# Issuing one tile's projections ahead of the previous tile's recurrence in a delta-rule attention layer

## What is computed

```python
q = silu(x @ Wq); k = l2_norm(silu(x @ Wk)); v = x @ Wv      # x: layer-normed
gk = log_sigmoid(x @ Wf1 @ Wf2)                              # per feature
gamma = -sigmoid(x @ Wgamma)                                 # per head
a = k * gamma[..., None] * exp(gk)
def step(S, inp):                                            # one token, per head
    qt, kt, vt, at, gkt = inp
    S = S * exp(gkt)[..., None]
    sab = einsum('bhk,bhkv->bhv', at, S)
    S = S + kt[..., None] * (sab[..., None, :] + vt[..., None, :])
    return (S, einsum('bhk,bhkv->bhv', qt, S))
o = scan(step) * sigmoid(x @ Wog1 @ Wog2); attn = norm(o) @ Wo
h = silu(x @ w1) * (x @ w2); h = gelu(h @ h1); h = gelu(h @ h2); ffn = h @ w3
out = x0 + attn + ffn
```

## Time and profile before

| | us |
|---|---|
| median of two timed runs | 13573.28 (13356.49 and 13790.07) |
| the profiled execution, device time | 13088.1 |
| its span, slowest core (core 2) | 13086.6 |
| spans of the eight cores | 13047.5 to 13086.6 |

### The profile page before, as it was taken

One profiled execution on the slowest core, in us unless ns is written; L12 is line 12 of the kernel. 1 busy time (PEld: TensorE's weight loads), 2 busy tenths in 40 slices (PEclk: granted clock), 3 DMA queues, 4 the chain that ended last, 5 costly groups with the idle time before them and its releaser, 6 DMA issues.

```text
span 13086.6 us, 179913 instructions; the slowest of 8 cores (13047.5 to 13086.6 us)
## 1 busy us (share of the span) xinstructions
PE 9249.0 (71%) x54234; PEld 4170.1 (32%) x55296; DVE 2440.8 (19%) x7011; ACT 2919.9 (22%) x8979; POOL 252.6 (2%) x479
## 2 busy tenths in 40 slices
PE   2566666666656656656656656699799799799577
PEld 0223223223223223223223223344344344344223
DVE  5222222222222222222222222000000000000222
ACT  1223323323333333333333333101010000000000
POOL 0000000000000000000000000000000000000110
PEclk5555555555555555555555555799999899899788
DMA  2100000000000000000000000322322322322421
GB/s 56 27 13 11 15 13 11 15 13 10 15 13 10 15 13 11 15 13 11 14 13 10 14 15 10 90 57 58 97 57 58 95 58 58 96 58 59 112 86 58
DMA packets 355161, 482.25 MB, mean 37 GB/s; under 512 B 162705, under 2 KB 277394, under 8 KB 336850
## 3 DMA queue, kind: packets, MB, share of 16 engines
q0 software_dynamic: 45040, 201.91, 8.3%
q10 hardware_dynamic: 177122, 235.20, 5.5%
q1 hardware_dynamic: 132096, 33.56, 1.4%
HBM read 479.50 MB, written 125.83 MB: 46 GB/s over the span
## 4 chain that ended last, share of the span: by engine, by line
PE 63%; ACT 11%; issue 10%; DVE 10%; DMA 3%; ACTq 2%; DVEq 1%; another core or an unknown queue 0%; POOL 0%; SPq 0%; POOLq 0%
PE lh_ps0h2t L1027 7%; PE lh_ps0h1t L1027 7%; PE lh_ps1h2t L1027 7%; PE lh_ps1h1t L1027 7%; PE p_ps L512 6%; PE p_px L855 6%; PE p_ps L521 5%; PE p_ps L560 3%; PE f_pF L1148 3%; PE p_pg L829 2%; ACT p_sumb L898 2%; DMA p_fmp<-p_pack 2%; DVE p_S L948 1%; DVE p2l_h L538 1%; ACT p2l_t L532 1%
## 5 line engine op out<-in xcount | busy, mean ns | idle before, releaser
L512 PE MATMUL p_ps<-xn_fm,p2l_wbb 128*128 128x512 bf16 x1775 | 1074.5, 605 | 375.9 <-DMA p_fmp<-p_pack 319.3
L521 PE MATMUL p_ps<-xn_fm,p2l_wbb 128*128 128x512 bf16 x1681 | 1023.2, 609 | 0.0
L1027 PE MATMUL lh_ps0h1t<-lh_hblkh1t,lh_wbbh1t 128*128 128x512 bf16 x4014 | 902.9, 380 | 150.4 <-DMA lh_hblkh1t<-h_dram 145.8
L1027 PE MATMUL lh_ps0h2t<-lh_hblkh2t,lh_wbbh2t 128*128 128x512 bf16 x4014 | 905.2, 381 | 140.5 <-DMA lh_hblkh2t<-g_dram 135.8
L1027 PE MATMUL lh_ps1h2t<-lh_hblkh2t,lh_wbbh2t 128*128 128x512 bf16 x4014 | 899.8, 379 | 4.4
L1027 PE MATMUL lh_ps1h1t<-lh_hblkh1t,lh_wbbh1t 128*128 128x512 bf16 x4014 | 899.8, 379 | 4.3
L863 ACT CAST p_xw<-p_px 128x128 bf16<-128x128 f32 x1280 | 340.6, 266 | 2011.7 <-PE p_px L855 2011.7
L1114 DVE TENSOR_SCALAR f_stats<-f_pS 1x512 f32<-1x512 f32 x8 | 5.4, 679 | 4087.1 <-DMA f_g2b<-h_dram 3915.2
L841 DVE CAST p_pow<-p_pg 128x128 bf16<-128x128 f32 x1280 | 373.2, 292 | 1989.8 <-PE p_pg4b L833 1989.8
L1027 PEld LDWEIGHTS lh_ps0h1t<-lh_hblkh1t,lh_wbbh1t 128*128 128x128 bf16 x4096 | 401.8, 98 | 631.4 <-issue 151.0
L1027 PEld LDWEIGHTS lh_ps0h2t<-lh_hblkh2t,lh_wbbh2t 128*128 128x128 bf16 x4096 | 402.4, 98 | 623.7 <-issue 144.6
(11 more groups left out here) (205 smaller groups left out, 12897.4 us busy)
## 6 DMA issues: line engine op xcount, KB each, us to landing
lh_wbbh1t<-h1t POOLq DMA_DIRECT2D x64, 1024.0 KB, 9.1
lh_wbbh2t<-h2t POOLq DMA_DIRECT2D x64, 1024.0 KB, 9.2
h_dram<-p2l_h ACTq DMA_DIRECT2D x256, 128.0 KB
lh_hblkh1t<-h_dram ACTq DMA_DIRECT2D x64, 512.0 KB
g_dram<-lh_gouth1t ACTq DMA_DIRECT2D x256, 128.0 KB
lh_hblkh2t<-g_dram ACTq DMA_DIRECT2D x64, 512.0 KB
h_dram<-lh_gouth2t ACTq DMA_DIRECT2D x256, 128.0 KB
f_g2b<-h_dram POOLq DMA_DIRECT2D x256, 128.0 KB, 5.3
```

The costliest lines, as they stand in the source:

```text
L512: kb.emit("tensor", lambda e, dc=dc, t0=t0, first=(dc == 0): e.matmul(ps4[:, 0:512], l1_wbb[:, dc * 128: dc * 128 + 128], xn[:, dc * T + t ...
L521: kb.emit("tensor", lambda e, dc=dc, t0=t0, first=(dc == 0): e.matmul(ps4[:, 512:1024], l1_wbb[:, 1024 + dc * 128: 1024 + dc * 128 + 128], ...
L1027: kb.emit("tensor", lambda e, dc=dc, b=b, pb=pb, ts=ts, TT=TT, first=(dc == 0): e.matmul(psb[pb][:, :], wbb[:, b * 4096 + dc * 128:b * 409 ...
```

## The change

The body of the tile loop is cut in two functions, `prologue(tk4)`, which returns the DT count of the transpose, and `waves(tk4, dtf)`. A new loop at the end of the segment calls them with the prologue one tile ahead. No instruction is added or removed, and no buffer is added. The order of the parts in a segment becomes head, P0, P1, W0, P2, W1, P3, W2, W3. The guards in `fr` are filled in at the time of each call, so their counts follow the new order.

```diff
-        for tk4 in range(TPS):
+        def prologue(tk4):
             tk = s * TPS + tk4
             tb = tk % 2
             t0 = tk * 128
...
             kb.emit("sync", lambda e, tb=tb: e.dma_start_transpose(
                 fmp[:, tb * 4096:(tb + 1) * 4096].rearrange("p (m r) -> p m r", r=128),
                 pack[:, tb * 4096:(tb + 1) * 4096]),
                 waits=[("V", vpack), ("A", apack)] + W(fr["fmpc"][tb]), inc="DT")
-            dtf = kb.cnt["DT"]
+            return kb.cnt["DT"]
+
+        def waves(tk4, dtf):
+            if dtf is None:
+                return
+            tk = s * TPS + tk4
+            tb = tk % 2
             kb.wait("tensor", [("DT", dtf)])
...
             fr["pack"][tb] = [("T", kb.cnt["T"]), ("DT", kb.cnt["DT"])]
             fr["fmpc"][tb] = [("T", kb.cnt["T"]), ("V", kb.cnt["V"]), ("G", kb.cnt["G"])]
             fr["gkb"] = [("T", kb.cnt["T"])]
+
+        dtn = {0: prologue(0)}
+        for tk4 in range(TPS):
+            if tk4 + 1 < TPS:
+                dtn[tk4 + 1] = prologue(tk4 + 1)
+            waves(tk4, dtn[tk4])
         vlast = kb.cnt["V"]
```

More of the change, by code:

```diff
@@ L601, in phase_p2 @@
             if P2_TSEC < 1:
-                continue
+                return None
             tq = projgrp(tk, 0, 512, bG(), fr["psG"])
```

## The result

| | before | after |
|---|---|---|
| median of the timed runs, us | 13613.8 (26 runs) | 13221.3 (29 runs) |
| lowest and highest | 13095.6 and 13915.4 | 12819.0 and 13640.9 |
| ratio of comparable runs | | 0.9802, interval 0.9735 to 0.9869 |
| profiled execution: spans of the cores | 13047.5 to 13086.6 | 12773.6 to 13165.5 |

The account below looks back on a forecast made before the run. The prediction took TensorE's 21.6 us wait for the transposed tile in each `p2` tile as the addressable bound; 3 x 8.2 + 9.1 - 1.8 + 1.3 = 33.2 us per segment, eight times, gave 12,822 us, range 12,740 to 13,340.

Parts of the forecast that it names:

- The transpose leaves the path, the tail stays: Between prologue and waves: TensorE's transpose wait (690.8 us in total) goes; ScalarE's and VectorE's closing work, 14.3 us, still delays the waves.
- P then W, 8.2 us: Where waves follow a prologue, three times per segment: the first mask starts right after L742, 8.2 us earlier, 197 us in all.
- P0 then P1, e + 40.6: Two prologues back to back, once per segment: the second ends 40.6 us after TensorE's last matmul of the first (e), gaining 9.1.
- The second start of the clock: Inside P1, after TensorE stands for 9 us: matmuls restart at the low clock, costing 2.2 us, bounds 0 and 9.
- W2 then W3, 1.8 us lost, 1.3 won: Two waves parts back to back, once per segment: exposed weight panel reload loses 1.8 us, a saved ScalarE table load wins 1.3.
- the 2 us that the prediction named as a sign: Expected in the changed trace: eight times L512 waits about 2 us for the weight panel `p2l_wbb` at a tile's start, ahead of W3.
- The sum, 266 us less, ratio 0.980: Whole kernel: 33.2 us gained per segment, eight times, 266 us off the profiled 13088.1, giving 12,822 us, ratio 0.980.
- The low clock in all prologues: Rival: TensorE's clock stays at 0.5 in every prologue, 56 matmuls taking 23.0 us; 67 us slower than before, 13,155 us; chance 4%.
- The halved gain: Rival: P1's 40 matmuls run at low clock and transposes slow the waves' first pair by 3 us; gain 140 us; chance 10%.
- The whole gap: Rival: ScalarE and VectorE take the waves' work before the next prologue's tail, so TensorE loses all 690.8 us; 12,397 us; chance 3%.

Follow-up runs that it names:

- the last three edits: Changed kernel with two halves of qtmp (no ratio on record), with the tail recorded inside the waves (0.9599 to the kernel before), and with both (0.9585).

## Why the prediction was right, and where it was wrong

*The transpose leaves the path, the tail stays.* Right. The wait on `p_fmp` is gone and the mask follows L742 without a pause; the two kernels with a second transpose and the one with a longer tail show both halves of the statement.

*P then W, 8.2 us.* In tile 1 the mask starts 14.0 us after the prologue's end instead of 22.2: 8.2 us. The transpose costs the first pair nothing, as taken: the pair's length and the kernel with two transposes show it. The reason given for it was weak, though. A share of 0.03 of the DMA engines was read in a stretch of waves without a transpose. With one, from 461.80 to 468.80 on core 0, it is 0.80. What held is that this load does not slow the waves, and no row before the change could tell that.

*P0 then P1, e + 40.6.* Measured e + 41.0, so the gain in this segment is 8.7 us and not 9.1. The second start of the clock was put at 2.2 us and came to 2.7: the 40 matmuls took 10.08 us after a stop of 9.5 us and 7.40 after one of 1.5. The stop was 9.5 us, the table load in it 1.28, as taken. What the prediction says of the load's price in the Trainium skill ("ScalarE: Activation LUTs", What ACT_TABLE_LOAD costs) needs a correction: the section gives about 1283 ns for the load, and reaches some 2.7 us with a drain of the engine. The rows have the 1.28 us and no drain: on core 0 before, ScalarE ends L905 at 445.95, loads from 446.03 and starts L532 at 447.32.

*W2 then W3, 1.8 us lost, 1.3 won.* The first tick of W3 started at 1120.74, 1.7 us after VectorE's last operation of W2 (L960) could have let it go (1118.94 and a handoff of 0.1). The wait itself is 4.0 us each (31.8 in 8), not the 2 us that the prediction named as a sign, since TensorE waits 2.4 us for L960 behind any waves (38.5 in 16 at L560). The table load was saved: between W2 and W3 none appears on ScalarE ahead of L532.

*The sum, 266 us less, ratio 0.980.* Right. The end of `p2` is 270 us earlier in the mean of the cores, and this is what bears on the sum. The measured ratio is 0.9802, but its interval allows any gain from 171 to 347 us of 13,088, so it is chance that it meets the forecast to the third digit. The fastest core in the trace is 274 us lower (13,047.5 to 12,773.6), and the lowest time of the changed kernel, whose eight clocks were alike as in the profiled execution before, is 12,819 us, where the sum said 12,822.

*The time itself.* Here a step failed. The median is 13,221 us, 399 above the predicted 12,822, and only the wide upper end of the range reaches it. The step is the sentence that made the sum against the profiled execution's 13,088 and then set the predicted time there, while the two timed runs stood 2.0% and 5.4% above it. I noted that their median less 266 is 13,307, and let it widen the range instead of moving the value. Against the median shown, 12,822 reads as a change of 5.5%, and against the later median of 13,614 as 5.8%, neither of which any term of the sum supports; the medians moved by 2.9%. What the runs show in its place: the profiled execution was one with no slowed core, its eight clocks being equal to 0.001. In only one of the 29 runs after the change (12,819 us) was that so. The term that was missing is thus no part of the change: it is the time by which the slowest of eight cores exceeds the fastest, 378 us in the median of those 30 executions of the changed kernel and 364 us in eleven of the kernel before, and it belonged on both sides. 13,307 would have been 0.7% off. What lowers the clock of some cores stays open.

*The spread.* The medians fell by 392 us and the fastest cores by 274. Whether the other 118 us are chance, or the changed kernel is slowed less often, is not settled. Chance is large enough for it: the kernel before had a median of 13,614 us in its 26 runs and of 13,442 in eleven others, run beside the last three edits.

*The rivals.* None came true. The low clock in all prologues did not come: behind the waves of W0 the 56 matmuls of P2 took 12.99 us on core 0, where the rival had 23.0. The halved gain did not come: P1's 40 matmuls lost 2.7 us and not 9, and the transposes cost the first pair nothing. The whole gap did not go, and the kernel with the tail inside the waves shows why: only the order of the lists held it.

## What to carry to other kernels

In this kernel, issuing a stage one step ahead hid only what no engine's own list put in front of the old work. Moving the whole prologue ahead took the DMA off the path and left the 14 us of ScalarE and VectorE work where they were; recording these in the idle places of the waves gained nearly as much again (229 us on top of 270). Price such a reordering by joint (which two parts meet, and which list item stands between them), and count the joints. And for a program on eight cores, state a sum as a ratio, and carry it to the median only after looking at how far the runs stand above the profiled execution.

## What the runs showed of the hardware

TensorE's clock after a stop. In P1 the 40 matmuls behind a stop of 9.5 us had a granted clock of 0.50 (1.2 GHz) in their first 5 us and a mean of 0.93 in the next 5; behind a stop of 1.5 us they had 1.00 (2.4 GHz) throughout. Stretches of core 0, of the changed kernel and then of the one with two halves of `qtmp`:

```profile
423.30:428.30 5.00, 5.00 (x12) 1.70 (x13) 0.00 (x0) 1.12 (x2) 0.00 (x0) 0.50 0.96 177
428.30:433.30 5.00, 5.00 (x29) 2.29 (x27) 0.85 (x2) 0.60 (x1) 0.00 (x0) 0.93 0.00 0
```

```profile
414.90:422.30 7.40, 7.38 (x40) 3.29 (x40) 5.99 (x9) 1.72 (x3) 0.00 (x0) 1.00 0.02 5
```

The difference is 2.7 us in this segment, and 2.5 in the mean of all eight (10.0 against 7.5 us for the 40). The Trainium skill ("TensorE: Matmul & The Clock Gate", Part 1: the throttled clock is the default, activity releases it, idleness brings it back) agrees with both rows.

Cores of one chip can part in the dense stages. In the execution profiled after the change, the matmuls of the first hidden layer took 379 to 381 ns on core 0 and 433 to 435 on core 6, those of the second 379 to 381 on both. Lines of the groups, core 0 first:

```profile
L1039 PE MATMUL lh_ps1h1t<-lh_hblkh1t,lh_wbbh1t 128*128 128x512 bf16 x4096 | 904.9, 379 | 0.0
```

```profile
L1039 PE MATMUL lh_ps1h1t<-lh_hblkh1t,lh_wbbh1t 128*128 128x512 bf16 x4096 | 1092.8, 435 | 0.0
```

From 8300 to 9500 us the granted clock was 0.97 on core 0 and 0.80 on core 6. In the profiled execution before, where all eight cores ran the same stages, none was slowed. The stages behind `p2` thus took 359 us longer on core 6 than on core 0, more than the change under study won, and such differences are what put the predicted time beside the median. Their cause was not looked for.
